# A decoder's cross-attention rearranged: relative context from memory, scores in eight array blocks, probabilities normalised on GpSimd, one ring of four banks

## The chip, the cores and the metric

One core of one Trainium2 chip runs the whole program. It has TensorE (PE, with its weight loads as PEld), VectorE (DVE), ScalarE (ACT), GpSimd (POOL) and SyncE (SP), whose queue issues the DMAs. The metric is the device time of the program in microseconds (us). Each engine takes its instructions in their written order and waits on semaphores; the engines run beside each other.

## The reference

The reference is a chain of twelve blocks on a state x of 32 sequences with 32 queries and 256 features, and a context of 32 sequences with 257 keys. The change lies in block four, a decoder of six layers, and in a preparation that it puts into block one. Each decoder layer is self-attention over 32 queries, cross-attention over the 257 keys and an MLP, each with a residual and a layer norm:

```
def proj(x, w, b):
    y = x @ w + b
    ...
q = proj(xq, W[0], B[0])
k = proj(xkv, W[1], B[1])
v = proj(xkv, W[2], B[2])
score = jnp.einsum('bhqd,bhkd->bhqk', q, k) / math.sqrt(DH)
attn = jax.nn.softmax(score, axis=-1)
out = jnp.einsum('bhqk,bhkd->bhqd', attn, v)
```

There are 16 heads of 16 features. All is float32.

## The kernel before

**The decoder's pipeline.** The 32 sequences lie in NG = 8 tiles of GB = 4 sequences (128 rows of queries). Six layers by eight tiles make 48 positions. The outer loop (decoder_layers, L2092) takes 51 steps; in step s the self-attention of position s, the projections ("prep": queries q, keys K, values V) of position s-1, the cross-attention of position s-2 and the output projection, norm and MLP of position s-3 are worked on together. A step has U = 8 units, u0 to u7, and the table UNIT_JOBS says which jobs PE does in which unit: S0, S1q, S1k, S2, S3, S6, S7 are self-attention, Y is the cross-attention's output projection, D0 to D3 are the MLP, n is a transpose. X and XK are done once a layer for the last key. Each job writes one bank of a ring of four PSUM banks (RING, RB = 4), ACT or DVE empties it, and job n waits until job n-4 has been emptied.

**Cross-attention.** A unit is one sequence and half of the heads. In each even unit `scores` makes the scores of two units (a pair) in banks 0 and 1; DVE takes their maxima (`maxima`), ACT takes four exponentials with their sums (`exponentials`). Two units later PE transposes the probabilities into a bank of its own (TURN), ACT copies that bank to pT (`copy_transposed`), and in odd units `values` multiplies with V into bank PV. The 257th key is kept out of the 256-key tiles: its part is handled by subtracting its key from the others (a bias less_last on K) and by its own share. After every fourth unit DVE computes the reciprocals of the sums and spreads them over a 512-wide tile (`reciprocals`), PE turns that into per-query factors with eight records of matmul (the L2363 matmuls), and DVE applies them to the heads (`own_heads`, five instructions).

**Order.** The DVE's order inside a unit is written out in its loop: jobs put off from the unit before (S3, D3), maxima, self_shares in u4, the unit's jobs, reciprocals, own_heads, own_queries in u2, self_shift in u3, then the second half of a layer norm (norm_apply), which waits for POOL's power of -1/2. A layer norm's first half (norm_statistics) empties the bank with its first instruction. POOL does nothing in the decoder but two tiny instructions a norm. ACT takes the first job of an even unit ahead of the exponentials.

**Names.** mm is a matmul, tr a transpose through PE. A float32 matmul shows as two PE records. ps is PSUM in eight banks; E.ctx holds two tiles of context, E.h the state.

```
[("D2", 1, "act"), ("X", None, "act")],
[("S7", None, "dve"), ("D3", None, "dve")],
```

These are u6 and u7 of the table.

## Time and profile before

| what | us |
|---|---|
| median of 3 runs | 4367.97 (4359.14 to 4368.52) |
| the profiled execution, first to last instruction | 4363.9 |
| PE busy in it | 3907.7 (90%) |
| DVE busy | 2607.3 (60%) |
| ACT busy | 1849.2 (42%) |
| POOL busy | 308.2 (7%) |

The profiled span lies 4.1 us under the median. The first self-attention transpose of the decoder starts at 718.11 us and its last MLP matmuls at 2716.80 us, so the decoder is the longest block, nearly half of the time. Busy time of PE overlaps between neighbours, because matmuls are pipelined; the distance between two starts tells what a job costs there.

### The profile page before, as it was taken

What the parts mean: (1) busy time and instruction counts of PE and PEld (TensorE: products, weight loads), DVE (VectorE), ACT (ScalarE), POOL (GpSimd) and SP (SyncE); (2) the same over time, 40 slices, a digit from 0 to 9 for tenths busy, and PEclk for the clock granted to TensorE, in tenths of its full rate; (3) what the DMA queues carried; (4) which work ended last, traced back from release to release, by engine and by line L of the source; (5) the groups of instructions that cost most, each with busy time, mean ns of one, the idle gap of its engine ahead of it and who ended that gap; (6) DMA issues with size and microseconds to landing.
All of it is one profiled execution on the core that took longest, in us unless ns stands there. A gap on an engine that the chain in (4) does not pass through costs nothing. (4 is left out here: it accounts for less than half of the span.)

```text
span 4363.9 us, 103007 instructions
## 1 busy us (share of the span) xinstructions
PE 3907.7 (90%) x43004; PEld 2910.7 (67%) x43004; DVE 2607.3 (60%) x5439; ACT 1849.2 (42%) x5103; POOL 308.2 (7%) x560
## 2 busy tenths in 40 slices
PE   7988995999999999999999997859678879889867
PEld 6765984677777777777777776548545569555535
DVE  3436113777777777777877775641156757346535
ACT  1221321455444544545445444312166736246523
POOL 0000101000000000000000000020111100000000
PEclk9999997999999999999999999969899979899978
DMA  4110484001111111111101100028654410000000
GB/s 155 60 63 3 152 301 158 30 31 52 50 35 48 50 36 47 51 34 48 59 26 47 60 21 11 11 82 288 213 165 146 156 44 1 26 30 30 11 1 12
DMA packets 116924, 310.60 MB, mean 71 GB/s; under 512 B 29352, under 2 KB 75624, under 8 KB 92016
## 3 DMA queue, kind: packets, MB, share of 16 engines
q1 hardware_dynamic: 113392, 295.61, 19.9%
q0 software_dynamic: 3072, 8.39, 0.5%
q8 instruction: 345, 5.65, 0.5%
q14 instruction: 115, 0.94, 0.1%
HBM read 289.01 MB, written 14.94 MB: 70 GB/s over the span
## 5 line engine op out<-in xcount | busy, mean ns | idle before, releaser
L2578 ACT COPY layers_pT<-banks 128x512 f32<-128x512 f32 x384 | 227.3, 592 | 554.5 <-PE banks L2346 553.8
L2277 PE MATMUL banks<-weights_a,ctx_tiles 128*128 128x256 f32 x1536 | 363.8, 380 | 0.0
L2270 PE MATMUL banks<-ctx_tiles,weights_a 128*128 128x512 f32 x768 | 363.4, 596 | 0.0
L2571 ACT ACTIVATE layers_probs<-banks,layers_negmax 128x256 f32<-128x256 f32 x768 | 354.2, 480 | 13.9 <-DVE layers_negmax L2436 6.8
L2277 PEld LDWEIGHTS banks<-weights_a,ctx_tiles 128*128 128x128 f32 x1536 | 285.9, 191 | 75.8 <-issue 46.4
L2414 DVE TENSOR_TENSOR layers_V<-banks,rows_a 128x512 f32<-128x512 f32 x192 | 132.7, 691 | 221.2 <-PE banks L2277 217.2
L2346 PE MATMUL banks<-const,layers_probs 128*128 128x128 f32 x1536 | 244.6, 282 | 2.8 <-ACT layers_pT L2578 2.8
L2346 PEld LDWEIGHTS banks<-const,layers_probs 128*128 128x128 f32 x1536 | 171.6, 141 | 106.4 <-issue 96.5
L2435 DVE TENSOR_REDUCE layers_negmax<-banks 128x4 f32<-128x1024 f32 x192 | 233.8, 1218 | 4.0 <-PE banks L2338 3.9
L2538 ACT ACTIVATE layers_KT<-banks,layers_less_last 128x256 f32<-128x256 f32 x384 | 162.1, 480 | 157.1 <-PE banks L2270 157.1
L2338 PE MATMUL banks<-layers_KT,layers_qblk 32*64 32x256 f32 x3072 | 211.3, 389 | 0.0
L2270 PEld LDWEIGHTS banks<-ctx_tiles,weights_a 128*128 128x128 f32 x768 | 132.1, 192 | 92.7 <-issue 92.6
L2321 PE MATMUL banks<-layers_dm_nT,weights_b 128*128 128x128 f32 x1536 | 190.0, 278 | 0.6 <-ACT layers_dm_nT L2533 0.6
L2321 PEld LDWEIGHTS banks<-layers_dm_nT,weights_b 128*128 128x128 f32 x1536 | 181.9, 195 | 0.9 <-ACT layers_dm_nT L2533 0.9
L2326 PE MATMUL banks<-weights_b,layers_hid 128*128 128x256 f32 x768 | 176.9, 384 | 3.8 <-ACT layers_hid L2561 3.1
L2326 PEld LDWEIGHTS banks<-weights_b,layers_hid 128*128 128x128 f32 x768 | 142.7, 190 | 36.6 <-issue 18.2
L2571 ACT ACTIVATION_READ_ACCUMULATOR layers_probs<-banks,layers_negmax 128x1 f32 x768 | 162.6, 212 | 0.0
L2338 PEld LDWEIGHTS banks<-layers_KT,layers_qblk 32*64 32x64 f32 x3072 | 98.6, 132 | 73.5 <-issue 40.6
L2561 ACT ACTIVATE layers_hid<-banks,layers_dm_cols 128x128 f32<-128x128 f32 x384 | 110.5, 379 | 62.3 <-PE banks L2321 62.2
L2358 PE MATMUL banks<-layers_pT,layers_V 128*32 128x64 f32 x6144 | 125.5, 222 | 6.1 <-ACT layers_pT L2578 6.1
L2859 PE MATMUL banks<-weights_a,ctx_tiles 128*128 128x512 f32 x256 | 127.2, 625 | 2.5 <-ACT l2x_nT L3083 1.5
L2358 PEld LDWEIGHTS banks<-layers_pT,layers_V 128*32 128x32 f32 x6144 | 96.2, 110 | 46.8 <-issue 40.0
(715 smaller groups left out, 8268.5 us busy)
## 6 DMA issues: line engine op xcount, KB each, us to landing
ctx_tiles<-in_ctx SPq DMA_DIRECT2D x65, 1028.0 KB, 5.3
weights_a<-in_L_w SPq DMA_DIRECT2D x44, 1024.0 KB, 5.5
l2x_B<-positions SPq DMA_DIRECT2D x32, 1280.0 KB, 5.9
weights_b<-in_L_w SPq DMA_DIRECT2D x32, 1024.0 KB, 6.2
weights_c<-in_L_w SPq DMA_DIRECT2D x16, 1024.0 KB, 7.1
weights_b<-in_L_xattn_w SPq DMA_DIRECT2D x12, 1024.0 KB, 7.4
l0x_key_rows<-in_ctx_rows SPq DMA_DIRECT2D x32, 256.0 KB, 2.6
ctx_tiles<-in_ctx_keys SPq DMA_DIRECT2D x32, 256.0 KB, 2.7
```

The source lines that it names most:

```text
L2270: last = mm(o.rearrange("p (j k) -> p j k", j=2), ca_wk[:, c, m * P:(m + 1) * P], keys, start=c == 0, stop=c == DC - 1)
L2277: last = mm(o[:, b * D:(b + 1) * D], E.ctx[:, tile % 2, c, first:first + P], ca_wv[:, c], start=c == 0, stop=c == DC - 1)
L2321: last = mm(o[:, i * P:(i + 1) * P], dm_w1[:, c, m * P:(m + 1) * P], dm_nT[:, c], start=c == 0, stop=c == DC - 1)
L2326: last = mm(o[:, 0:D], hid[:, m], dm_w2[:, m], start=m == 0, stop=m == FC - 1)
L2338: last = mm(ps[half, r // 2, a * KW:(a + 1) * KW], qblk[rows, tile % 2, cc, j + a], KT[rows, tile % 2, cc, (j + a) * KW:(j + a + 1) * KW], ...
L2346: last = tr(ps[:, TURN, (KC * t + c) * P:(KC * t + c + 1) * P], probs[:, cc, j, t, c * P:(c + 1) * P], E.c("ident"))
L2358: last = mm(ps[32 * i:32 * (i + 1), PV, j * 64:(j + 1) * 64], V[:, pos % 2, KC * j + c, cc * P + 32 * i:cc * P + 32 * (i + 1)], pT[:, k % ...
L2414: last = v.tensor_tensor(V[:, tile % 2, KC * arg:KC * (arg + 1)], o.rearrange("p (b d) -> p b d", b=KC), E.rA[:, 0].unsqueeze(1).to_broadc ...
L2435: link(v.tensor_reduce(peak, ps[:, 0:2].rearrange("p t (a x) -> p t a x", a=2), AX.X, ALU.max, negate=True))
L2538: last = a(KT[:, pos % 2, m, j * KW:(j + 1) * KW], o[:, j % 2 * KW:(j % 2 + 1) * KW], ACT.Identity, bias=less_last[:, pos // NG % 2, m, se ...
L2571: a(probs[:, cc, i, t], ps[:, t, i % 2 * KW:(i % 2 + 1) * KW], ACT.Exp, bias=negmax[:, cc, t, i:i + 1], accum_out=totals[:, cc, t, i:i + 1 ...
L2578: nc.scalar.copy(pT[:, k % 4].rearrange("p t c x -> p (t c x)"), ps[:, TURN]).then_inc(s["copied"], 1)
```

## The change

Five things are done together.

- The relative context. In block one (joint_attention) POOL subtracts the last key from the 256 others, tile by tile (less_last), and SP writes the result to a scratch tensor in memory (ctx_rel). The decoder loads its tiles from there, from step 0 on. The bias less_last of K and its job XK go, K is emptied by one instruction of 512 columns instead of two of 256, and V is copied without a bias row, since the values are relative too.
- The scores. The four strips of 32 rows write four banks, and the two sequences of a pair write the two halves of the rows, so that the eight matmuls of a pair have eight blocks of the array (4 strips by 2 halves), where before they had four, used twice.
- The normalising. For every pair DVE adds and inverts the sums (pair_rates) and POOL multiplies the probabilities with them before they are transposed (scale, twice a pair). The spread tile, its matmuls and the two multiplications of the heads go; own_heads is two instructions of half the width, once a pair.
- The ring. The scores have banks 0 to 3; transposes (T) and values (PV) become jobs of the ring of four banks 4 to 7 with all other jobs. A PV is emptied by DVE in the next unit, behind the maxima.
- POOL's order is written out anew: the roots of the norms stand between the scales.

```diff
-                    if K >= GB and K % GB == 1:
+                    if K % GB == 3:
+                        g = K // GB
+                        sp.wait_ge(s["rel_ready"], g + 1)
+                        sp.dma_start(E.ctx_rel[g], rel[:].rearrange("p c j k -> p c (j k)")).then_inc(s["rel_stored"], 16)
+                    if K >= GB and K % GB == 1 and (K + 3) // GB < NG:
...
+                    tile = E.ctx[:, g % 2].rearrange("p c (j k) -> p c j k", j=GB)
+                    for c in range(DC):
+                        last = nc.gpsimd.tensor_tensor(rel[:, c], tile[:, c, :, 1:LK], tile[:, c, :, 0:1].to_broadcast([P, GB, KW]), ALU.subtract)
+                    last.then_inc(s["rel_ready"], 1)
...
-    TURN, PV, RING, RB = 2, 3, 4, 4
+    RING, RB = 4, 4
...
         for step, parts in enumerate(steps):
             for u in range(U):
+                it = step * U + u
+                if ca_unit(it - 2):
+                    at[it - 2 - 2 * U, "T", None] = len(jobs)
+                    jobs.append((step, u, "T", it - 2, "act"))
                 for kind, arg, engine in UNIT_JOBS[u]:
...
+                if u % 2 and ca_unit(it - 3):
+                    at[(it - 3) // 2 - U, "PV", None] = len(jobs)
+                    jobs.append((step, u, "PV", it - 3, "dve"))
...
-                        sp.dma_start(E.ctx[:, step % 2], A["ctx"][step % NG]).then_inc(s[f"ctx{step % 2}"], 16)
+                        sp.dma_start(E.ctx[:, step % 2, :, 0:GB * KW], E.ctx_rel[step % NG]).then_inc(s[f"ctx{step % 2}"], 16)
...
                     need(pe, "exp_done", 2 * k)
+                    for r in range(4):
+                        rows = slice(32 * r, 32 * (r + 1))
+                        for a in range(2):
+                            last = mm(ps[64 * a:64 * (a + 1), r, 0:KW], qblk[rows, tile % 2, cc, j + a], KT[rows, tile % 2, cc, (j + a) * KW:(j + a + 1) * KW], start=True, stop=True)
+                    last.then_inc(s["scores_done"], 1)
+
+                def transposes(o, k, pos, cc, j):
+                    pe.wait_ge(s["scaled"], k + 1)
...
-                        for r in (0, 2, 1, 3):
-                            rows, half = slice(32 * r, 32 * (r + 1)), slice(64 * (r % 2), 64 * (r % 2 + 1))
-                            last = mm(ps[half, r // 2, a * KW:(a + 1) * KW], qblk[rows, tile % 2, cc, j + a], KT[rows, tile % 2, cc, (j + a) * KW:(j + a + 1) * KW], start=True, stop=True)
...
+                    link(v.scalar_tensor_tensor(blend[:], both[:, :, 0], E.c("pairmask")[:, 0:1], last_share, ALU.mult, ALU.add))
+                    v.scalar_tensor_tensor(attnT[:, cc, j * LQ:(j + 2) * LQ].rearrange("p (j q) -> p j q", j=2), both[:, :, 1], E.c("pairmask")[:, 1:2], blend[:], ALU.mult, ALU.add).then_inc(s["evac_dve"], 1)
...
                     for a in put_off:
-                        take(*a)
-                    put_off.clear()
+                        if a[3] != "PV":
+                            take(*a)
                     if it % 2 == 0 and ca_unit(it):
                         maxima(*ca_unit(it))
+                    for a in put_off:
+                        if a[3] == "PV":
+                            take(*a)
+                    put_off.clear()
                     if u == 4 and steps[step]["sa"] is not None:
                         self_shares(steps[step]["sa"])
+                    if it % 2 and ca_unit(it - 1):
+                        pair_rates(*ca_unit(it - 1))
...
+                def scale(k, pos, cc, j):
+
+                    pool.wait_ge(s["rates_ready"], k // 2 + 1)
+                    at = slice(2 * (j % 2), 2 * (j % 2) + 2)
+                    nc.gpsimd.tensor_tensor(probs[:, cc, j // 2, at], probs[:, cc, j // 2, at], rates[:, cc, j // 2, at].unsqueeze(2).to_broadcast([P, 2, KW]), ALU.mult).then_inc(s["scaled"], 1)
+
+                for it in range(N * U + 1):
+                    step, u = it // U, it % U
+                    if u == 0 and step and steps[step - 1]["dm"] is not None:
+                        root("dm")
+                    if u == 2 and step < N and steps[step]["out"] is not None:
+                        root("ca")
+                    if u == 7 and steps[step]["sa"] is not None:
+                        root("sa")
+                    if it % 2 and ca_unit(it - 1):
+                        scale(*ca_unit(it - 1))
+                        scale(*ca_unit(it))
```

**DVE from u7 into u1, before.** y_sa is the norm behind S7, y_dm the norm behind D3, negmax the maxima, V the emptying of job V.

```order
L2385 TENSOR_TENSOR layers_y_sa<-banks,rows_c 128x256 [waits layers_job_done]
...
L2396 TENSOR_SCALAR layers_y_sa<-layers_y_sa,layers_stats_sa 128x256 [waits layers_power_ready]
...
L2385 TENSOR_TENSOR layers_y_dm<-banks,rows_b 128x256 [waits layers_job_done]
...
L2435 TENSOR_REDUCE layers_negmax<-banks 128x2x2 [waits layers_scores_done]
...
L2414 TENSOR_TENSOR layers_V<-banks,rows_a 128x512 [waits layers_job_done]
L2441 TENSOR_TENSOR layers_rates<-layers_totals,layers_last_e 128x2x4 [waits layers_last_exp,layers_exp_done]
```

The same place now; blend and attnT are own_heads, rates is pair_rates.

```order
L2462 TENSOR_TENSOR layers_rates<-layers_totals,layers_last_e 128x4 [waits layers_last_exp,layers_exp_done]
...
L2401 TENSOR_TENSOR layers_y_sa<-banks,rows_c 128x256 [waits layers_job_done]
...
L2401 TENSOR_TENSOR layers_y_dm<-banks,rows_b 128x256 [waits layers_job_done]
...
L2454 TENSOR_REDUCE layers_negmax<-banks 128x4 [waits layers_scores_done]
...
L2472 SCALAR_TENSOR_TENSOR layers_blend<-banks,const,layers_last_v 128x64 [waits layers_job_done]
...
L2433 COPY layers_V<-banks 128x512 [waits layers_job_done]
```

A wait for the exponentials of the same unit pair now stands ahead of the norm of S7, and the emptying of PV stands between the maxima and V.

**PE from u7 into u0, now.** Line 2372 is the transposes T, 2353 is D3, 2383 is PV, 2365 the scores, 2302 is K, 2309 is V.

```order
L2353 MATMUL banks<-weights_b,layers_hid 128x256 [waits layers_evac_act]
...
L2383 MATMUL banks<-layers_pT,layers_V 32x64 [waits layers_evac_act]
...
L2365 MATMUL banks<-layers_KT,layers_qblk 64x256 [waits layers_exp_done,layers_evac_act,layers_qblk_ready]
...
L2372 MATMUL banks<-const,layers_probs 128x128 [waits layers_scaled,layers_evac_act]
...
L2302 MATMUL banks<-ctx_tiles,weights_a 128x512 [waits layers_ctx0,layers_evac_dve]
...
L2309 MATMUL banks<-weights_a,ctx_tiles 128x256 [waits layers_evac_dve]
```

T now waits for POOL (layers_scaled), K for the emptying of D3 and V for that of PV, both by DVE; before, T waited for the exponentials and for its own bank.

**POOL, one step, now.**

```order
L188 TENSOR_SCALAR layers_stats_sa<-layers_stats_sa 128x1 [waits layers_var_ready]
L193 TENSOR_TENSOR layers_stats_sa<-layers_stats_sa,const 128x1 [waits layers_added_eps]
L2539 TENSOR_TENSOR layers_probs<-layers_probs,layers_rates 128x512 [waits layers_rates_ready] x2
L188 TENSOR_SCALAR layers_stats_dm<-layers_stats_dm 128x1 [waits layers_var_ready]
L193 TENSOR_TENSOR layers_stats_dm<-layers_stats_dm,const 128x1 [waits layers_added_eps]
```

The two scales of the last pair of a step stand behind the root of S7's norm.

## Rows read from the trace of the kernel before

**Rows 1.** Busy time by engine (PE, PEld, DVE, ACT, POOL), clock, DMA, one decoder step.
```profile
1499.60:1540.02 40.42, 40.40 (x459) 29.72 (x459) 31.51 (x70) 20.12 (x66) 2.48 (x6) 1.00 0.09 28
```

**Rows 2.** Timeline of PE: start, us, line, operation, records; the same step.
```profile
1504.05 1.06 PE L2262 MATMUL banks<-layers_sa_nT,weights_c 128*128 128x128 f32 x8
...
1507.87 0.66 PE L2358 MATMUL banks<-layers_pT,layers_V 128*32 128x64 f32 x32
1508.34 0.61 PE L2363 MATMUL banks<-layers_spread,const 128*32 128x256 f32 x8
1508.88 1.09 PE L2338 MATMUL banks<-layers_KT,layers_qblk 32*64 32x256 f32 x16
1509.91 0.66 PE L2346 MATMUL banks<-const,layers_probs 128*128 128x128 f32 x4
...
1513.98 1.07 PE L2301 MATMUL banks<-weights_a,layers_sa_k 128*32 128x256 f32 x16
...
1523.05 1.03 PE L2295 MATMUL banks<-weights_c,layers_sa_nT 128*128 128x256 f32 x4
...
1533.17 0.60 PE L2346 MATMUL banks<-const,layers_probs 128*128 128x128 f32 x4
...
1534.65 3.69 PE L2326 MATMUL banks<-weights_b,layers_hid 128*128 128x256 f32 x16
1538.28 0.66 PE L2358 MATMUL banks<-layers_pT,layers_V 128*32 128x64 f32 x32
1538.86 1.09 PE L2338 MATMUL banks<-layers_KT,layers_qblk 32*64 32x256 f32 x16
1539.88 0.66 PE L2346 MATMUL banks<-const,layers_probs 128*128 128x128 f32 x4
...
1542.31 1.89 PE L2277 MATMUL banks<-weights_a,ctx_tiles 128*128 128x256 f32 x8
```

**Rows 3.** Timeline of DVE in the same step.
```profile
1504.42 0.16 DVE L2441 TENSOR_TENSOR layers_rates<-layers_totals,layers_last_e 128x8 f32<-128x8 f32 x1
...
1504.85 0.17 DVE L2443 TENSOR_TENSOR layers_rates<-layers_rates,layers_last_e 128x8 f32<-128x8 f32 x1
...
1505.66 0.41 DVE L2396 TENSOR_SCALAR layers_y_dm<-layers_y_dm,layers_stats_dm 128x256 f32<-128x256 f32 x1
...
1506.91 2.47 DVE L2410 SCALAR_TENSOR_TENSOR weights_a<-banks,layers_sa_cols,const 128x1024 f32<-128x1024 f32 x2
...
1519.12 0.69 DVE L2414 TENSOR_TENSOR layers_V<-banks,rows_a 128x512 f32<-128x512 f32 x1 [0.41 <-PE banks L2277]
...
1521.87 1.22 DVE L2435 TENSOR_REDUCE layers_negmax<-banks 128x4 f32<-128x1024 f32 x1
...
1534.67 0.42 DVE L2385 TENSOR_TENSOR layers_y_sa<-banks,rows_c 128x256 f32<-128x256 f32 x1 [1.34 <-PE banks L2314]
...
1537.23 0.41 DVE L2396 TENSOR_SCALAR layers_y_sa<-layers_y_sa,layers_stats_sa 128x256 f32<-128x256 f32 x1 [0.99 <-POOL layers_stats_sa L193]
...
1538.48 0.41 DVE L2385 TENSOR_TENSOR layers_y_dm<-banks,rows_b 128x256 f32<-128x256 f32 x1
...
1540.02 1.22 DVE L2435 TENSOR_REDUCE layers_negmax<-banks 128x4 f32<-128x1024 f32 x1
```

**Rows 4.** Timeline of ACT: the end of the exponentials of the last pair.
```profile
1536.18 0.25 ACT L2573 ACTIVATE layers_last_e<-layers_negmax 128x8 f32<-128x8 f32 x1
```

**Rows 5.** POOL by line and form: count, busy us, mean ns, idle before.
```profile
L3033 POOL TENSOR_TENSOR ctx_tiles<-ctx_tiles 128x512 f32<-128x512 f32 x32 | 37.2, 1183 | 40.8 <-DMA ctx_tiles<-in_ctx_keys 40.7 <-DMA ctx_tiles<-in_ctx_last 0.2
```

**Rows 6.** Timeline of POOL and DVE in block seven, side by side.
```profile
3228.20 4.34 POOL L3033 TENSOR_TENSOR ctx_tiles<-ctx_tiles 128x512 f32<-128x512 f32 x3
3228.27 1.12 DVE L182 TENSOR_SCALAR l2x_n<-x_state,l2x_stats 128x256 f32<-128x256 f32 x1 [1.00 <-POOL l2x_stats L193]
...
3275.77 3.04 POOL L3033 TENSOR_TENSOR ctx_tiles<-ctx_tiles 128x512 f32<-128x512 f32 x3
```

**Rows 7.** Timeline of PE early in the decoder.
```profile
806.37 0.43 PE L2358 MATMUL banks<-layers_pT,layers_V 128*32 128x64 f32 x16 [2.22 <-ACT layers_pT L2578]
806.73 1.98 PE L2338 MATMUL banks<-layers_KT,layers_qblk 32*64 32x256 f32 x16
```

More of the change, by code:

```diff
@@ L2447, in own_heads, with pair_rates @@
-                def own_heads(k, pos, cc, j):
+                def pair_rates(k, pos, cc, j):
+                    dve.wait_ge(s["exp_done"], 2 * k + 4)
+                    dve.wait_ge(s["last_exp"], k // 2 + 1)
+                    rate = rates[:, cc, j // 2]
+                    link(v.tensor_tensor(rate, totals[:, cc, j // 2], last_e[:, cc, j // 2], ALU.add))
+                    v.reciprocal(rate, rate).then_inc(s["rates_ready"], 1)
+                def own_heads(o, n, k, pos, cc, j):
                     tile = pos % NG
-                    dve.wait_ge(s["pv_done"], k + 1)
-                    dve.wait_ge(s["shares_done"], k // GB + 1)
-                    if k % (NG * U) == GB - 1:
+                    if k % (NG * U) == 0:
@@ L2513, in _, with root @@
             def _(pool):
-                n = 0
-                for parts in steps:
-                    for part, kind in (("out", "ca"), ("sa", "sa"), ("dm", "dm")):
-                        if parts[part] is not None:
-                            power(E, pool, s, n, stats[kind][:, 8:9], stats[kind][:, 7:8], 1e-12)
-                            n += 1
+                made = [0]
+                def root(kind):
+                    power(E, pool, s, made[0], stats[kind][:, 8:9], stats[kind][:, 7:8], 1e-12)
+                    made[0] += 1
+                def scale(k, pos, cc, j):
[13 more added lines that the diff above has]
+                        scale(*ca_unit(it))
             @blk.scalar
@@ L2582, in _ @@
                     early = 0
-                    if ca_unit(it - 2):
-                        copy_transposed(*ca_unit(it - 2))
                     if it % 2 == 0 and ca_unit(it):
-                        while jobs_in(it)[early:early + 1] and early < 1 + (jobs_in(it)[0][3] == "XK"):
-                            take(*jobs_in(it)[early])
-                            early += 1
+                        early = 1 + (jobs_in(it)[0][3] == "T")
+                        for b in jobs_in(it)[0:early]:
+                            take(*b)
                         exponentials(*ca_unit(it))
```

196 lines of the change are left out of this document (85 added, 111 removed).

## The prediction

> **What bounds the kernel now.** I read the busy time by stretch first. In a decoder step of 40.42 us PE is busy 40.40, DVE 31.51, ACT 20.12 and POOL 2.48, with the full clock [rows 1]. So PE alone sets the step; what matters is the distance between two PE starts. The decoder has 45 steps in which all four parts are at work (steps 3 to 47), each of this length. Then I read PE, DVE and ACT of that step by time, because the order on DVE and the four banks decide whether PE can keep its pace. The reader is to see in [rows 2, 3] that PE has no gap, and that DVE is ahead of PE in u7 (it waits 1.34 us for S7) but behind it elsewhere: it starts the maxima of u4 at 1521.87, and PE has been at the next work for a while.
>
> **PE work that goes.** The spread matmuls cost 1508.88 - 1508.34 = 0.54 us, twice a step: 1.08 [rows 2]. The scores cost 1509.91 - 1508.88 = 1.03 us, four times a step [rows 2]. They are 16 records of 256 columns in four blocks. D3's 16 records of the same length in the whole array take 1538.28 - 1534.65 = 3.63, or 0.227 each [rows 2]; a quarter of that is 0.91, so 0.12 of the 1.03 is change-over. Eight blocks need 0.45 + 0.12, about 0.6. The bounds are 0.6 and 1.03 (no gain); I take 0.6, since four blocks already come to a quarter, here and in S3. That saves 4 x 0.43 = 1.72. All of this is on the path. With no new wait the step is 40.4 - 2.8 = 37.6 us. T and PV have as many records as before. XK is six small jobs and counts as nothing.
>
> **DVE, ACT, POOL.** DVE loses two reciprocals with spread a step, 1505.66 - 1504.42 = 1.24 each [rows 3], and two own_heads of five instructions of 128x128, each 0.3 by the same bounds as below: about 5.5. It gains four pair_rates of 0.43 (1504.42 to 1504.85 is an add and a reciprocal [rows 3]) and four own_heads of about 0.6 (two instructions of 128x64, each between the 0.16 of 8 elements and the 0.41 of 256; I take 0.3). That is 1.4 less. But it has to be there at certain times. POOL gets eight scales a step. The nearest rows are 32 subtractions of the same form, mean 1.18 us, and three in a row take 3.04, so 1.04 each when alone [rows 5, 6]. ACT has fewer instructions for K and two more last_e; it has 20 us to spare.
>
> **A walk through the step.** I set t = 0 at the start of the scores in u0 and carry every wait on. Hand-overs to PE count 0.15.
>
> *The last pair.* D2 ends 1538.86 - 1533.17 = 5.69 before the scores. The last exponential of u6 ends at 1536.43 [rows 4], 3.26 behind D2: t = -2.4. pair_rates waits for this, ahead of S7 in DVE's order, and ends at -2.0; before, DVE was at S7 already. From the start of S7's statistics to the second half of the norm is 1537.23 - 1534.67 = 2.56 [rows 3]: root done at 0.5. POOL's scale of unit 6 stands behind that root and runs 0.5 to 1.55. PE is at T at 0.6 and waits until 1.65: **1.1 us**.
>
> *The shared access.* The three instructions of the norm start at the same moment as the scales. [Rows 6] show what then happens: a tensor_scalar of 128x256 takes 1.12 us instead of the 0.41 of [rows 3], as it ends just behind the POOL instruction, and three POOL instructions take 4.34 instead of 3.04. So they take turns: scale 6, tensor_scalar to 1.65, scale 7 to 2.65, the other two to 3.45. The norm alone would take 1538.48 - 1537.23 = 1.25 and end at 1.8.
>
> The Trainium skill (SBUF — State Buffer, Who interferes with whom) says that a DVE instruction with two SBUF inputs, or in a two-port mode, and a GpSimd instruction that reads SBUF exclude each other for the whole instruction. By that rule the trace agrees; without it, with each at its own length, the step would be 42.7 instead of 44.6 (worked out below).
>
> *K and V of u0.* K0 needs D3's bank, four jobs back, emptied by the first instruction of its statistics at 3.45 + 0.42. PE would be there at 1.65 + 0.7 = 2.4 and starts at 4.0: **1.6 us**. The statistics end at 5.0 (1540.02 - 1538.48 = 1.54), the maxima with their clamp at 6.4, own_heads at 7.0. V0 needs the bank of PV. PE would be there at 4.0 + 1.7 = 5.7 and starts at 7.15: **1.4 us**.
>
> *u1.* V0 ends at 8.9. DVE copies it (0.85 with hand-over), does the MLP's norm (1.25), pair_rates (0.43) and S1q's emptying (2.47): 13.9. PV in u1 is four jobs behind S1q. PE would be there 0.44 for T and 1507.87 - 1504.05 = 3.82 behind V0, at 13.15: **0.9 us**.
>
> *u4.* S2 is four jobs behind the PV of u3. From the end of Y to S2 PE needs 1523.05 - 1513.98 less the 0.43 of the scores: 8.6. DVE needs 0.1 + 2.56 + 1.25 for Y's norm, 0.8 for S3, 0.43 for the rates, 0.65 for V2, 2.2 for the shift (V2 to maxima is 1521.87 - 1519.12 = 2.75 in all [rows 3]), 1.4 for the maxima and 0.6 for own_heads: 10.0, and 0.15. That is 1.5 us of wait; two of the shift's instructions meet the scales, which adds about 0.3, and T of u4 waits 0.25 for its scale: **2.0 us**.
>
> Waits: 1.1 + 1.6 + 1.4 + 0.9 + 2.0 = 7.0 us against 2.8 saved. The step is 40.4 + 4.2 = **44.6 us**. Over 45 steps this is 45 x 4.2 = 189 us. The steps at the ends lack either self-attention or keys and have slack of their own; I count them as nothing, within 10 us.
>
> Without the taking of turns the waits are 1.1 + 0 + 1.5 + 0.9 + 1.6 = 5.1, the step 42.7, and the sum 45 x 2.3 = 104 us.
>
> **What costs nothing.** In block one 16 POOL subtractions of 128x1024, some 2 us each by twice the form of [rows 5], lie beside PE, which sets that block's pace; POOL has only a root for each tile there, and the next root stands ahead of each subtraction. SP's new wait for rel_ready stands ahead of the loads of key rows, which are three deep, and eight stores of 1 MB go out in some 260 us. Without that cover it would be 8 x 4 us. The decoder's first context load is now issued with step 0 and used some 20 us later. At step ends the same SP queue as before loads weights; its share is 0.09 [rows 1]. I take 0, and up to 15 us for the upper end.
>
> **Rivals.**
> 1. *The waits without taking turns.* For: POOL's two short instructions beside DVE in a decoder step cost almost nothing now. Against: [rows 6]. 4368 + 104 = 4472.
> 2. *The scores stay at 1.03.* For: no row has 32*64 tiles of 256 columns in eight blocks. Against: the quarter above. Half of the lost 1.72 hides behind DVE (in u0 and u4, where PE waits anyway), so 45 x 0.86 = 39 more: 4596.
> 3. *The clock falls.* After a gap of 2.22 us the scores took 1.98 instead of 1.09, at 1.2 instead of 2.4 GHz [rows 7]. If the gaps of u0, 4 us in 7, do this once a step, some 2 us are added: 45 x 2 = 90 more, 4647. Against: my single gaps are all under 2.
> 4. *Faster.* DVE, with 1.4 us less work, is early enough at one place, the run from S7 in u7 to S1q in u1. If the norm of S7, the maxima and PV come early there, the banks are free when PE arrives. It decides at a shortening of that run by about 5 us, the sum of its four waits. Then PE keeps nearly all of the 2.8: 4368 - 126 = 4242. For: DVE would be busy 30 of 37.6 us only. Against: the run is a chain, with the exponentials and a root of 1.0 us in it, that no spare time elsewhere shortens.
> 5. *A draw.* The waits come to 2.8 by being half as long as I say: 4368.
>
> **How the numbers follow.** The profiled span is 4363.9, 4.1 under the median; I add the change to the median: 4368 + 189 = 4557. Chances: forecast 0.40, rival 1 0.24, rival 2 0.07, rival 3 0.07, rival 4 0.15, rival 5 0.07. The range from 4400 to 4640 holds the forecast and rivals 1 and 2 with their ends, and leaves out rivals 4 and 5 and most of 3. About 0.2% (9 us) is what a measurement of this kernel can tell. Faster 0.15, same 0.06, slower 0.79.
>
> **What would show it.** Right: a decoder step of 44 to 45 us with PE busy some 38; PE idle before T in u0 by POOL, and before K0, V0, PV of u1 and S2 by DVE; scores 0.6 us apart from T; the norm of S7 stretched from 1.25 to nearly 3 us beside two scales. The walk is wrong if PE's gaps sum to under 3 us a step, if the rates of the last pair are done before S7 ends, or if a scale takes other than 1.0 to 1.2 us where DVE is quiet. If the stretch is missing, rival 1 holds.

## The result and the profile after

The changed kernel takes 4499.31 us, the median of 4 runs (4494.44 to 4504.27), against 4368.25 (4359.14 to 4370.86) for the kernel before on the same chip: a ratio of 1.0307, 95% interval [1.0296, 1.0319]. The change makes the kernel 131 us slower. The profiled execution has a span of 4492.7 us, 128.8 more than before. The forecast was 4557, the range 4400 to 4640.

The first two lines of the profile's page after, and then two full decoder steps by stretch (length; busy PE, PEld, DVE, ACT, POOL; granted clock; DMA share), which answer to [rows 1]:

```profile
span 4492.7 us, 101679 instructions
...
PE 3846.5 (86%) x42188; PEld 2843.7 (63%) x42188; DVE 2577.7 (57%) x5343; ACT 1824.7 (41%) x4995; POOL 729.7 (16%) x960
```
```profile
1506.43:1550.48 44.05, 40.37 (x449) 28.80 (x442) 30.68 (x66) 19.69 (x64) 10.64 (x15) 0.96 0.32 106
1550.48:1593.98 43.50, 38.84 (x450) 28.23 (x443) 30.67 (x66) 19.69 (x64) 10.65 (x15) 1.00 0.08 25
```

PE was busy for the whole step before. Now it is idle for 4.7 us of 43.5 in the second step, which has the full clock. The first lost clock (0.96) and is 0.55 us longer. From the scores of u0 in step 3 to those in step 48 a step is 43.67 us on average, where it was 40.62: 3.05 x 45 = 137 us. The rest of the difference lies elsewhere: the decoder's first PE instruction comes 7.2 us later than before, the steps at the decoder's ends give 5 back, and what follows its last MLP matmuls is 10 us shorter (1637 instead of 1647). The change touches nothing there, and in the traces of all the kernels below this part takes between 1637 and 1651 us, so these 10 us are no effect that is shown.

The second step on PE (start, duration, in brackets the idle time and its releaser), which answers to [rows 2]:

```profile
1550.48 0.69 PE L2365 MATMUL banks<-layers_KT,layers_qblk 32*64 32x256 f32 x16
1552.09 0.63 PE L2372 MATMUL banks<-const,layers_probs 128*128 128x128 f32 x4 [0.92 <-POOL layers_probs L2539]
1552.56 0.38 PE L2288 MATMUL banks<-const,h_state 128*128 128x128 f32 x2
1554.12 1.98 PE L2302 MATMUL banks<-ctx_tiles,weights_a 128*128 128x512 f32 x4 [1.18 <-DVE layers_y_dm L2401]
1557.08 1.99 PE L2309 MATMUL banks<-weights_a,ctx_tiles 128*128 128x256 f32 x8 [0.97 <-DVE layers_attnT L2473]
...
1563.74 0.65 PE L2383 MATMUL banks<-layers_pT,layers_V 128*32 128x64 f32 x32 [0.51 <-DVE weights_a L2429]
1564.33 0.69 PE L2365 MATMUL banks<-layers_KT,layers_qblk 32*64 32x256 f32 x16
1564.94 0.66 PE L2372 MATMUL banks<-const,layers_probs 128*128 128x128 f32 x4
...
1575.96 1.88 PE L2302 MATMUL banks<-ctx_tiles,weights_a 128*128 128x512 f32 x4
1578.90 1.13 PE L2322 MATMUL banks<-weights_c,layers_sa_nT 128*128 128x256 f32 x4 [1.05 <-DVE layers_attnT L2473]
```

These are the only waits of the step: T, K0 and V0 of u0, PV of u1, S2 of u4. The brackets sum to 4.6 us. The distances between starts say more. From each I take the distance of the same two jobs in a kernel without these waits (below, "and ScalarE's order"). S0 to K0, for one, is 1.56 here and 0.22 there. By this T waits 1.00 us, K0 1.35, V0 1.24, PV 0.58 and S2 1.22, in all 5.4. The scores stand 1564.94 - 1564.33 = 0.61 us ahead of T, where it was 1.03.

DVE in the same step, which answers to [rows 3], with POOL's two scales:

```profile
1548.16 0.16 DVE L2462 TENSOR_TENSOR layers_rates<-layers_totals,layers_last_e 128x4 f32<-128x4 f32 x1 [3.35 <-ACT layers_last_e L2603]
...
1548.45 0.40 DVE L2401 TENSOR_TENSOR layers_y_sa<-banks,rows_c 128x256 f32<-128x256 f32 x1
...
1550.97 1.12 DVE L2412 TENSOR_SCALAR layers_y_sa<-layers_y_sa,layers_stats_sa 128x256 f32<-128x256 f32 x1 [1.00 <-POOL layers_stats_sa L193]
1552.13 1.14 DVE L2413 TENSOR_TENSOR layers_y_sa<-layers_y_sa,rows_c 128x256 f32<-128x256 f32 x1
1553.31 0.42 DVE L2414 TENSOR_TENSOR h_state<-layers_y_sa,rows_c 128x256 f32<-128x256 f32 x1
1553.65 0.42 DVE L2401 TENSOR_TENSOR layers_y_dm<-banks,rows_b 128x256 f32<-128x256 f32 x1
...
1555.12 1.19 DVE L2454 TENSOR_REDUCE layers_negmax<-banks 128x4 f32<-128x1024 f32 x1
```
```profile
1550.91 2.08 POOL L2539 TENSOR_TENSOR layers_probs<-layers_probs,layers_rates 128x512 f32<-128x512 f32 x2
```

DVE waits 3.35 us for the last exponential, although the bank of S7, its next piece of work, has been full since 1546.3, when PE ended this:

```profile
1545.23 1.03 PE L2341 MATMUL banks<-weights_c,layers_sa_attnT 128*128 128x256 f32 x4
```

So some 1.9 of the 3.35 us delay S7. Then the norm of S7 meets the scales. Its first two instructions take 1.12 and 1.14 us. Over the whole program those lines have a mean of 1090 and 1113 ns for this norm and of 413 and 425 for the norm behind Y, which meets no scale.

### The profile page after: what moved, and what is told of

The parts are those of the page before. It is cut to its first block and busy times, and to the rows that moved or that the text cites. A ratio compares the mean times of both kernels' runs of the same rounds, so it can differ in the third digit from the quotient of the medians.

```text
span 4492.7 us, 101679 instructions
## 1 busy us (share of the span) xinstructions
PE 3846.5 (86%) x42188; PEld 2843.7 (63%) x42188; DVE 2577.7 (57%) x5343; ACT 1824.7 (41%) x4995; POOL 729.7 (16%) x960
## 5 line engine op out<-in xcount | busy, mean ns | idle before, releaser
L2539 POOL TENSOR_TENSOR layers_probs<-layers_probs,layers_rates 128x512 f32<-128x512 f32 x384 | 393.3, 1045 | 694.3 <-DVE layers_rates L2463 694.3
L2302 PE MATMUL banks<-ctx_tiles,weights_a 128*128 128x512 f32 x768 | 390.9, 634 | 52.0 <-DVE layers_y_dm L2401 52.0
L2372 PE MATMUL banks<-const,layers_probs 128*128 128x128 f32 x1536 | 243.5, 282 | 43.7 <-POOL layers_probs L2539 42.4
L2433 DVE COPY layers_V<-banks 128x512 f32<-128x512 f32 x192 | 132.7, 691 | 244.7 <-PE banks L2309 241.4
L2579 ACT ACTIVATE layers_KT<-banks,layers_key_bias 128x512 f32<-128x512 f32 x192 | 132.7, 691 | 154.4 <-PE banks L2302 154.2
L2365 PE MATMUL banks<-layers_KT,layers_qblk 32*64 32x256 f32 x3072 | 133.4, 403 | 0.0
```

The costliest lines, as they stand in the source:

```text
L2302: last = mm(o, ca_wk[:, c, m * P:(m + 1) * P], E.ctx[:, tile % 2, c, 2 * i * KW:2 * (i + 1) * KW], start=c == 0, stop=c == DC - 1)
L2365: last = mm(ps[64 * a:64 * (a + 1), r, 0:KW], qblk[rows, tile % 2, cc, j + a], KT[rows, tile % 2, cc, (j + a) * KW:(j + a + 1) * KW], star ...
L2372: last = tr(o[:, (KC * i + c) * P:(KC * i + c + 1) * P], probs[:, cc, j // 2, 2 * (j % 2) + i, c * P:(c + 1) * P], E.c("ident"))
L2433: last = v.tensor_copy(V[:, tile % 2, KC * arg:KC * (arg + 1)], o.rearrange("p (b d) -> p b d", b=KC))
L2539: nc.gpsimd.tensor_tensor(probs[:, cc, j // 2, at], probs[:, cc, j // 2, at], rates[:, cc, j // 2, at].unsqueeze(2).to_broadcast([P, 2, KW ...
```

## The experiments

The times are medians of 4 runs (the last row 12); the ratio is to runs of the kernel before on the same chip, with its 95% interval. The kernel before took 4368 us on the chips of most rows and 4361.7 on that of "and ScalarE's order", "the same, four blocks" and the last row. The last column is the time in the trace from the first to the last MLP matmul of the decoder (D3), which is 47 steps.

| kernel | us | ratio to before | D3 to D3, us |
|---|---|---|---|
| before | 4368 | 1 | 1875.5 |
| the change | 4499.3 | 1.0307 [1.0296, 1.0319] | 2012.1 |
| GpSimd scales first | 4457.9 | 1.0213 [1.0196, 1.0231] | 1972.9 |
| S7 first | 4401.3 | 1.0080 [1.0064, 1.0097] | 1914.3 |
| no scaling | 4424.4 | 1.0132 [1.0114, 1.0150] | 1940.6 |
| fill instead of scaling | 4458.9 | 1.0209 [1.0191, 1.0226] | 1968.7 |
| scaling on ScalarE | 4435.6 | 1.0148 [1.0127, 1.0170] | 1943.2 |
| scores in four blocks | 4537.2 | 1.0395 [1.0375, 1.0416] | 2047.3 |
| new order on DVE | 4340.6 | 0.9942 [0.9924, 0.9960] | 1853.0 |
| and scaling on ScalarE | 4315.6 | 0.9886 [0.9868, 0.9905] | 1826.3 |
| and ScalarE's order | 4250.8 | 0.9735 [0.9714, 0.9756] | 1765.7 |
| the same, four blocks | 4328.9 | 0.9917 [0.9894, 0.9940] | 1836.2 |
| the same, scaling on GpSimd | 4302.0 | 0.9853 [0.9831, 0.9875] | 1814.6 |
| before, with block one's part | 4367.6 | 1.0007 [0.9996, 1.0018] | 1875.6 |

The theory from the prediction: the step is set by a run over DVE and POOL from S7 in u7 to the emptying of S1q in u1; it starts late, behind the rates, and is stretched by taking turns with the scales. The rivals: the change costs by work wherever it is done; the stretch has another cause; the clock does it.

### GpSimd scales first

```
                     if it % 2 and ca_unit(it - 1):
                         scale(*ca_unit(it - 1))
                         scale(*ca_unit(it))
+                    if u == 7 and steps[step]["sa"] is not None:
+                        root("sa")
```
(and `root("sa")` no longer ahead of the scales)

> The changed kernel with one order turned round: in unit 7 GpSimd scales the probabilities of units 6 and 7 first and takes the power for the self-attention's norm after them. Times are on the clock of one step of the changed kernel's trace (scores of unit 0 at 1550.48). The wait of the transposes for GpSimd (0.92 us a step) must go in every theory. Theory (GpSimd's scaling and VectorE's instructions with two operands in memory take turns): scaling now lies at 1548.5 to 1550.6, beside the statistics of S7 instead of the norm; those are stretched, the power is at 1551.5 to 1552.3, the norm ends at about 1553.7 as now, and the ring bank of D3, for which K waits, comes free no earlier: 0 to 15 us faster. Rival (no taking turns; the norm was long for another reason): statistics end at 1550.0, power at 1551.4, norm ends at 1552.8, V starts 0.8 us earlier, 45 x 0.8 = 36 us faster or more.

Measured: 41 us faster than the change. My number was wrong, and the rival's was right for a wrong reason. In the trace (start, duration) the scales now lie beside the statistics of S7:

```profile
1488.42 2.22 POOL L2539 TENSOR_TENSOR layers_probs<-layers_probs,layers_rates 128x512 f32<-128x512 f32 x2 [7.41 <-DVE layers_rates L2463]
1488.69 1.06 DVE L2403 TENSOR_TENSOR layers_y_sa<-layers_y_sa,h_state 128x256 f32<-128x256 f32 x1
1489.78 0.43 DVE L2404 BATCH_NORM_STATS2 layers_stats_sa<-layers_y_sa 128x6 f32<-128x256 f32 x1
```

They do get in each other's way: L2403, which adds two tiles in memory, takes 1.06 us instead of the 0.42 it has elsewhere, and the two scales 2.22 instead of 2.04. But that is the only one of the four statistics with both operands in memory. I had counted all four instructions of the statistics as stretched. V0 starts 5.89 us behind the scores instead of 6.60; 0.71 x 45 = 32 us, and 8 more come from the clock (below).

### S7 first

```
-                    if it % 2 and ca_unit(it - 1):
+                    if it % 2 and u != 7 and ca_unit(it - 1):
                         pair_rates(*ca_unit(it - 1))
                     for a in jobs_in(it):
...
+                    if u == 7 and ca_unit(it - 1):
+                        pair_rates(*ca_unit(it - 1))
```

> The changed kernel with one order turned round on VectorE: in unit 7 it takes the statistics of S7 (ready at 1546.3) before the rates of units 6 and 7, which wait for ScalarE's last exponential until 1548.16. Theory (the run from S7's statistics over the power, the norm, D3, the maxima to the values' bank sets V's start in unit 0, and everything in it is late because the statistics wait behind the rates): statistics 1546.5 to 1548.1, power done 1548.7, norm beside the scaling until 1551.6, D3's bank free at 1552.1, values' bank at 1555.1, V at 1555.3 instead of 1557.08: 1.8 us a step, 45 x 1.8 = 80 us faster, about 4420 us. Rival (ScalarE's or GpSimd's part, not the order on VectorE, sets the unit): V's start moves by under 0.4 us, under 18 us faster.

Measured: 98 us faster. This is the largest effect of one edit. The statistics start when PE has S7 ready, and the rates hardly wait:

```profile
1507.40 0.42 DVE L2401 TENSOR_TENSOR layers_y_sa<-banks,rows_c 128x256 f32<-128x256 f32 x1 [1.50 <-PE banks L2341]
...
1509.27 0.16 DVE L2462 TENSOR_TENSOR layers_rates<-layers_totals,layers_last_e 128x4 f32<-128x4 f32 x1 [0.30 <-ACT layers_last_e L2605]
...
1511.59 0.69 PE L2365 MATMUL banks<-layers_KT,layers_qblk 32*64 32x256 f32 x16
...
1516.07 1.99 PE L2309 MATMUL banks<-weights_a,ctx_tiles 128*128 128x256 f32 x8 [0.97 <-DVE layers_attnT L2473]
```

V0 starts 4.48 us behind the scores of u0 instead of 6.60, which is 95 us over 45 steps. The norm is as stretched as before (1.12 and 1.14 us); it only starts earlier. So the late start is worth more than the stretch: leaving the scales out, which takes away the stretch and T's wait, gives 75 us (next experiment). The waits of V0, PV and S2 remain.

### No scaling, and a fill in its place

The first leaves the scaling out. The second puts a fill of equal length in its place; in both the probabilities stay unnormalised.

```
-                    pe.wait_ge(s["scaled"], k + 1)
+                    pe.wait_ge(s["rates_ready"], k // 2 + 1)
```
```
-                    nc.gpsimd.tensor_tensor(probs[:, cc, j // 2, at], probs[:, cc, j // 2, at], rates[:, cc, j // 2, at].unsqueeze(2).to_broadcast([P, 2, KW]), ALU.mult).then_inc(s["scaled"], 1)
+                    if k:
+                        pool.wait_ge(s["scaled"], k)
+                    nc.gpsimd.memset(idle[:], 0.0).then_inc(s["scaled"], 1)
```

> The changed kernel without GpSimd's scaling of the probabilities: the 384 multiplications are left out and the transposes wait for the rates instead, so the probabilities stay unnormalised. Theory (taking turns stretches the norm from 1.25 to 2.7 us, and the norm stands ahead of D3's statistics and all that follows): no wait of the transposes in unit 0, norm 1.3 us, K at 1552.8, V at 1555.65 instead of 1557.08: 1.4 us a step, about 64 us faster. Rival (norm would be as long without the scaling): V's start stays, and only the wait in front of the transposes is handed to K: 0 to 10 us faster.

> The changed kernel with each of GpSimd's 384 scalings replaced by a fill of 1070 elements a partition on a tile of its own: about as long (the fill of 706 elements of block one took 0.686 us), with the same waits, but it reads nothing in memory; the probabilities stay unnormalised. It parts the duration of GpSimd's step from its reading. Theory (it is the reading and VectorE's two operands that exclude each other): the transposes still wait about 1 us in unit 0, but the norm is 1.3 us, and V starts at 1555.65: some 60 us faster, as without the scaling. Rival (any work of GpSimd on memory stretches the norm, or its length alone counts): norm 2.7 us as before, 0 to 10 us faster.

Measured: 75 us faster without scaling, 40 with the fill. The norm of S7 without scaling, then with the fill, where POOL's line stands first:

```profile
1523.52 0.41 DVE L2412 TENSOR_SCALAR layers_y_sa<-layers_y_sa,layers_stats_sa 128x256 f32<-128x256 f32 x1 [1.00 <-POOL layers_stats_sa L193]
1523.97 0.43 DVE L2413 TENSOR_TENSOR layers_y_sa<-layers_y_sa,rows_c 128x256 f32<-128x256 f32 x1
```
```profile
1494.87 2.10 POOL L2542 MEMSET layers_idle<- 128x1070 f32 x2
1494.96 1.05 DVE L2413 TENSOR_SCALAR layers_y_sa<-layers_y_sa,layers_stats_sa 128x256 f32<-128x256 f32 x1 [1.00 <-POOL layers_stats_sa L193]
...
1496.04 0.43 DVE L2414 TENSOR_TENSOR layers_y_sa<-layers_y_sa,rows_c 128x256 f32<-128x256 f32 x1
```

Nothing on POOL, no stretch: the cause is the scale. The fill, which reads nothing, still delays the tensor_scalar (1.05 us) but not the tensor_tensor with two operands in memory (0.43, while the second fill runs). So my expectation was half right: there are two ways of being in each other's way, and the fill leaves one of them. V0 starts 5.16 us behind the scores without scaling and 5.81 with the fill, against 6.60: 65 and 36 us, and in both some 8 more for the clock (below), so 73 and 44 of the 75 and 40 measured.

The Trainium skill (SBUF — State Buffer, Who interferes with whom) says that a DVE instruction with two SBUF inputs contends with a GpSimd instruction that reads SBUF and not with one that only writes. The tensor_tensor agrees: 1.14 us beside the scale, 0.43 beside the fill. Of a two-port mode, which it says a tensor_scalar can enter, it says that it contends with GpSimd, without that exception. The tensor_scalar's 1.12 and 1.05 us fit this; that it runs in such a mode no row here shows.

### The same work on ScalarE

```
+                def scale(k, pos, cc, j):
+                    act.wait_ge(s["rates_ready"], k // 2 + 1)
+                    for r in range(2 * (j % 2), 2 * (j % 2) + 2):
+                        last = a(probs[:, cc, j // 2, r], probs[:, cc, j // 2, r], ACT.Copy, scale=rates[:, cc, j // 2, r:r + 1])
+                    last.then_inc(s["scaled"], 1)
```
(called for both units of a pair at the end of an odd unit; POOL's is gone)

> The changed kernel in its own order, with the normalising alone moved from GpSimd to ScalarE (four copies with a scale per pair of units at the end of the odd units). All the work of the change is there, but GpSimd does none of it. Theory (the scaling costs by GpSimd's access to memory and by its place on the path, not by the work): as without any scaling, about 4424 us, 75 us faster than the change. Rival (the scaling costs wherever it is done): 4480 us or more.

Measured: 64 us faster than the change, most of the 75 us that leaving the scaling out gave. Four copies take 1.71 us together. The rival that the work costs wherever it is done falls: a full decoder step is 42.06 us long with the scaling on ScalarE and 42.06 without any, and the stretch from D3 to D3 differs by 2.6 us. Of the 11 us between the two times 9 lie behind the decoder in the two traces (1651 and 1642 us), where the kernels are the same.

### Scores in four blocks

```
+                            part = slice(32 * (2 * (r // 2) + a), 32 * (2 * (r // 2) + a + 1))
-                            last = mm(ps[64 * a:64 * (a + 1), r, 0:KW], qblk[rows, tile % 2, cc, j + a], KT[rows, tile % 2, cc, (j + a) * KW:(j + a + 1) * KW], start=True, stop=True)
+                            last = mm(ps[64 * a:64 * (a + 1), r, 0:KW], qblk[part, tile % 2, cc, j + a], KT[part, tile % 2, cc, (j + a) * KW:(j + a + 1) * KW], start=True, stop=True)
```
(which strip of rows a matmul takes now follows from the half that it writes, so the scores come out of the wrong rows)

> The changed kernel with the scores' matmuls spread over four blocks of the array instead of eight: the rows that a matmul takes are chosen by which half of the bank it writes, so two follow each other on every block; the scores are wrong by that, their number and size are not. It prices the eight blocks. The scores should take 1.03 us instead of 0.62. Theory (that time lies on the path in units 2 and 6 alone; in unit 0 it is hidden by the transposes' wait and in unit 4 by S2's): 2 x 0.41 x 45 = 37 us slower, about 4536 us. Rival (TensorE's time counts in full in each unit): 4 x 0.41 x 45 = 74 us slower, 4573 us. Rival (eight blocks are no faster than four): no difference.

Measured: 38 us slower. The scores are 1.03 us ahead of T again:

```profile
1531.07 1.11 PE L2366 MATMUL banks<-layers_KT,layers_qblk 32*64 32x256 f32 x16
1532.10 0.66 PE L2373 MATMUL banks<-const,layers_probs 128*128 128x128 f32 x4
```

Eight blocks do save 0.41 us, but only half of that shortens the step: in u0 and u4 PE would wait anyway. A step at the full clock is 44.33 us long instead of 43.49, which is two times 0.42. T's wait for POOL shrank from 42.4 to 23.6 us over the program, or 0.4 a step, which is what the scores grew by. That the total meets the 37 us expected so closely is partly luck: with T's wait shorter the clock fell in 4 steps instead of 17 (see rival 3 below), so the 45 full steps grew by 30 us only, and the rest lies outside them.

### A new order on DVE

```
                     for a in put_off:
-                        if a[3] != "PV":
-                            take(*a)
+                        take(*a)
+                    put_off.clear()
                     if it % 2 == 0 and ca_unit(it):
                         maxima(*ca_unit(it))
-                    for a in put_off:
-                        if a[3] == "PV":
-                            take(*a)
-                    put_off.clear()
+                    for a in unfinished:
+                        norm_apply(*a)
+                    unfinished.clear()
```
(and S7 ahead of the rates, as above)

> The changed kernel with VectorE's order written anew, nothing else: the statistics of S7 ahead of the rates in unit 7 (as in the run before), the values of every second unit taken out of their bank ahead of the maxima instead of behind them, and the norm behind D3 applied ahead of V's copy in unit 0, where VectorE waits for V anyway, instead of behind it. Theory (TensorE waits only because the ring banks are emptied late by VectorE): on top of the 98 us of the order in unit 7, the waits left in that trace go, V in unit 0 (1.2 us), PV in unit 1 (0.6) and S2 (1.1): 2.9 us x 45 = 130 us more, about 4270 us, faster than the kernel before by some 2%. Rival (each wait taken away uncovers another, such as the exponentials, which now start 0.6 us later, or the scores' banks): half of it at most, 4330 us or more.

Measured: 61 us faster than with S7 first alone, 27 faster than the kernel before (ratio 0.9942). All waits for DVE went, but the rival holds in part: the maxima of u0 end 4.4 us behind the scores instead of 3.9, so 0.5 us later, ScalarE's exponentials with them, and K's banks are emptied behind those. This edit moves two things beside S7 and takes three waits away (V0, PV, S2); which of the two took which is argued and not shown. Of PE in this kernel, K in u1 and V in u5:

```profile
1496.47 1.98 PE L2302 MATMUL banks<-ctx_tiles,weights_a 128*128 128x512 f32 x4 [0.55 <-ACT layers_KT L2580]
...
1517.30 1.99 PE L2309 MATMUL banks<-weights_a,ctx_tiles 128*128 128x256 f32 x8 [0.61 <-ACT layers_KT L2580]
```

### Scaling on ScalarE in the new order, and ScalarE's order

> The kernel of the run before with the normalising moved from GpSimd to ScalarE: four copies with a scale per pair of units, at the end of the odd units of ScalarE's order. Theory (GpSimd's scaling costs by stretching the norm beside it, and after the reordering only K's wait of 0.3 us in unit 0 is left of that): 5 to 15 us faster than with GpSimd, about 4255 us, if ScalarE's copies take 0.35 us each. Rival (ScalarE's queue becomes the late one: 4 x 0.35 us more in each odd unit, ahead of the next unit's evacuations): 10 to 50 us slower than with GpSimd.

Measured: 25 us faster than with the new order alone, more than expected. In unit 1 K's wait went, and T of u2 waits for its scaling instead; V in u5 waits as before:

```profile
1510.69 1.99 PE L2309 MATMUL banks<-weights_a,ctx_tiles 128*128 128x256 f32 x8 [0.61 <-ACT layers_KT L2571]
...
1533.44 0.63 PE L2372 MATMUL banks<-const,layers_probs 128*128 128x128 f32 x4 [0.45 <-ACT layers_probs L2600]
```

The next kernel moves two things on ScalarE:

```
-                        early = 1 + (jobs_in(it)[0][3] == "T")
+                        early = (2 if u == 4 else 1) + (jobs_in(it)[0][3] == "T")
```
(K's evacuation ahead of the exponentials in u4; and in u1 both `scale` calls directly behind the copy of T)

> The kernel with the new order on VectorE and the normalising on ScalarE, with two places of ScalarE's order changed: in unit 1 the scaling stands ahead of K's evacuation, in unit 4 K's evacuation stands ahead of the exponentials. In the trace of the run before, TensorE still waited for ScalarE in two places a step: 0.5 us ahead of the transposes of unit 2 (their scaling stood behind the evacuations of unit 1) and 0.8 us ahead of V in unit 5 (K's bank was emptied behind the exponentials). Theory: both go and nothing comes up, since ScalarE waits idle where the moved instructions now stand: 1.3 x 45 = 58 us faster, about 4257 us; TensorE busy for 37.6 us of a step of about 37.8. Rival (the exponentials or the maxima come up next): under 30 us faster.

Measured: 4250.8 us, 65 faster than the one before it, 2.65% faster than the kernel before and 5.5% than the change. Its step:

```profile
1495.92:1533.87 37.95, 37.93 (x450) 28.30 (x443) 29.61 (x67) 26.14 (x80) 2.48 (x6) 1.00 0.09 30
```

PE is busy for 37.93 of 37.95 us. All the arithmetic of the change is in this kernel; what differs from the change is the order on two engines and that ScalarE does the scaling.

### The same kernel with four blocks, and with GpSimd's scaling

> The kernel of the run before with the scores in four blocks of the array instead of eight, chosen by the half of the bank (the scores are wrong by that, number and size are not). In the changed kernel this cost 38 us, because half of the units hid it behind waits. Theory (without waits TensorE's time counts in full): 4 x 0.41 x 45 = 74 us slower than the kernel with eight blocks. Rival (the waits were not what hid it): 38 us again.

Measured: 78 us slower than with eight blocks, of 74 expected. Where PE waits for nothing its time counts in full, twice as much as in the change.

> The fastest kernel so far (VectorE's new order, K's evacuation of unit 4 ahead of the exponentials) with the normalising given back to GpSimd. It prices GpSimd's place beside VectorE where TensorE waits for nothing else. Theory (the scaling stretches the norm of S7 by 1.45 us, so the maxima of unit 0, the exponentials and K's evacuation behind them come later, and K of unit 1 waits 0.55 us for its bank, as in the trace of the new order with GpSimd; K of unit 0 waits 0.2): 0.75 x 45 = 34 us slower than with ScalarE, about 4285 us. Rival (with this order nothing is left of it): within 10 us of the kernel with ScalarE, 4251 us.

Measured: 51 us slower than with ScalarE. T's, V's and S2's waits stay away, and K of u1 waits:

```profile
1521.43 1.98 PE L2302 MATMUL banks<-ctx_tiles,weights_a 128*128 128x512 f32 x4 [0.56 <-ACT layers_KT L2580]
```

I had used the bracket as the price. By the distances between starts, against the kernel with ScalarE, K of u1 waits 0.73 us and K0 0.19. Each of these two K also takes 0.10 us longer to the next start (1.82 instead of 1.72). Together this is 1.1 us a step (39.06 instead of 37.95), or 50 of the 51 us.

### Block one's part alone

```
+                def less_last(g):
...
+                        last = nc.gpsimd.tensor_tensor(rel[:, c], tile[:, c, :, 1:LK], tile[:, c, :, 0:1].to_broadcast([P, GB, KW]), ALU.subtract)
```
(with the stores of `rel` and their waits, added to the kernel before)

> The kernel before, with the part of the change that lies in block one alone: GpSimd subtracts the last key (16 instructions) and SyncE stores the eight tiles, which nothing reads. The decoder is as before. Theory (block one's end came 6.9 us later in the changed kernel's trace, because GpSimd's power for the next norm stands behind less access to memory beside its subtractions, and TensorE lost the clock there): 7 us slower, 4375 us. Rival (what was later in block one is chance of the clock at its start): 0 to 2 us slower.

Measured: a ratio of 1.0007 [0.9996, 1.0018] over 12 runs, so between 2 us faster and 8 slower. It doesn't tell 7 us from none. In its one trace the decoder's first PE instruction is at 725.83 us, as in the changed kernel (725.3) and not as before (718.1). In the traces of all thirteen kernels with this part it lies between 723.5 and 731.7 us. That speaks for a delay of 5 us or more, but there is one trace only of the kernel before, and the times do not prove it.

## Why the prediction came out as it did

**Sign and mechanism were right.** The order of waits, their releasers and their places came out as listed. T's wait and most of K0's went with one exchange on DVE ("S7 first"), and those of V0, PV and S2 with two more, done together.

**PE work.** The scores came to 0.61 us instead of the 0.6 taken. The step without waits is 37.95, not 37.6. Most of the error is in the spread matmuls, priced at their own distance of 0.54 us [rows 2]; the scores' 4 x 0.41 instead of 4 x 0.43 is 0.08 of it. PV is followed by the spread after 1508.34 - 1507.87 = 0.47 us and by scores after 1538.86 - 1538.28 = 0.58 [rows 2], so leaving the spread out moves the scores by only 0.54 + 0.47 - 0.58 = 0.43, and 0.86 a step goes, not 1.08. With 4 x 0.41 this is 2.5.

**The last pair and the shared access.** From the scores at t = 0 the last exponential ended at -2.43 (-2.4 said), the rates at -1.95 (-2.0), the root at 0.46 (0.5), T started at 1.61 (1.65), the stretched norm ended at 3.25 (3.45).

**K0, V0, PV.** Starts at 3.64, 6.60 and 13.26, where I had 4.0, 7.15 and 14.05. The waits are 1.35, 1.24 and 0.58 instead of 1.6, 1.4 and 0.9. Each term was a little long: hand-overs on DVE overlap (D3's statistics start 0.08 us ahead of the norm's recorded end), and durations were added up with none of that.

**u4: the term that was mis-sized most.** 1.2 instead of 2.0. T did not wait, and the shift was not stretched, since what meets the scale in u3 is the copy under a mask and a reduction:

```profile
1574.77 0.79 DVE L2486 COPY_PREDICATED_SCALAR layers_sa_sc<-mask_zero,layers_floor 128x512 f32 x1
1575.59 0.69 DVE L2487 TENSOR_REDUCE layers_sa_max<-layers_sa_sc 128x16 f32<-128x512 f32 x1
1576.31 0.69 DVE L2488 TENSOR_TENSOR layers_sa_sc<-layers_sa_sc,layers_sa_max 128x512 f32<-128x512 f32 x1
```
```profile
1574.08 2.04 POOL L2539 TENSOR_TENSOR layers_probs<-layers_probs,layers_rates 128x512 f32<-128x512 f32 x2 [2.33 <-DVE layers_rates L2463]
```

The first takes 0.79 us here and a mean of 0.78 without any scaling, and the subtraction starts as the scales have ended. "Two of the shift's instructions meet the scales" was right, that it adds 0.3 was not. With T's 0.25 this is 0.55 of the 0.8; the rest I have not taken apart.

**The sum.** The waits are 5.4 instead of 7.0 and the savings 2.5 instead of 2.8. V0 and S2, which start behind a wait, also take 0.1 us longer each to the next start, which no term had. So a step at the full clock grew from 40.42 to 43.49, by 3.07. Two more terms were missing. The lost clock adds 0.18 to the average step. And the prediction's "each of this length" is wrong for 6 of the 45 steps of the kernel before. Step 3, with its lost clock, took 42.04 us, and in five steps X and XK come on top, eight records each. Here are step 8 and, with them, step 9:

```profile
1010.46:1050.89 40.43, 40.41 (x466) 29.73 (x459) 31.50 (x69) 20.13 (x66) 2.47 (x6) 1.00 0.33 93
1050.89:1092.75 41.86, 41.86 (x481) 31.51 (x474) 31.25 (x69) 21.48 (x72) 2.48 (x6) 1.00 0.08 27
```

These six add 0.20 us to the average step before. In the change step 3 is no longer than the others (43.47), XK is gone, and a step with X is 0.6 us longer and the next one 0.6 shorter (44.07 and 42.90 at the full clock), so nothing of the 0.20 is left. XK with X, counted as nothing, was worth 5 x 1.44 = 7 us. In all 3.07 + 0.18 - 0.20 = 3.05 us a step instead of 4.2, so 137 instead of 189 us.

**Rival 1** is refuted by the norm's rows, with the scales and without them. Its time (4472) was nearer to the 4499 measured than mine (4557), so the total does not speak for the taking of turns; it had the waits too small and missed the clock, where mine had them too large. **Rival 2** is refuted by the 0.61. **Rival 3** happened, but small. I argued that my single gaps are all under 2 us; the clock fell behind gaps of 0.92 and 1.18 us. In the step at 1506.43 the granted clock was 0.60 from 1510 to 1514 and K took 3.10 us instead of 1.98, that is, part of it ran at 1.2 instead of 2.4 GHz:

```profile
1508.04 0.63 PE L2372 MATMUL banks<-const,layers_probs 128*128 128x128 f32 x4 [0.92 <-POOL layers_probs L2539]
...
1510.07 3.10 PE L2302 MATMUL banks<-ctx_tiles,weights_a 128*128 128x512 f32 x4 [1.18 <-DVE layers_y_dm L2401]
1513.02 2.56 PE L2309 MATMUL banks<-weights_a,ctx_tiles 128*128 128x256 f32 x8
```
```profile
1510.00:1514.00 4.00, 3.93 (x6) 1.66 (x7) 2.79 (x8) 1.50 (x7) 0.79 (x2) 0.60 0.00 0
```

V0 would have started at 1513.03 anyway, so K's 1.12 us were hidden and the step grew by only 0.55. The clock fell in 17 of the 45 full steps, and the average step is 0.18 above the full-clock one: 8 us in all, where the rival had 90. With GpSimd scaling first, with S7 first, without scaling and with the fill the clock is at 1.00 from step 4 to step 47, so each of these got some 8 us on top. **Rival 4** did not happen, but its counter-argument was wrong. I wrote that the run from S7 is a chain that no spare time elsewhere shortens. Exchanging two steps on DVE shortened it by 2.1 us a step. Of the 248 us between the change and the kernel of 4251 us, 197 came from the order on DVE and ScalarE and 51 from the place of the scaling.

**What costs nothing.** SP's waits and the context loads show no wait of PE. Block one's part was taken as 0. It is 7 us in two traces against one, and not certain in the times.

## What to carry over

Work taken off the bound engine pays only where no other engine's order decides, so walk the others' order against the new pace and look for an instruction that waits at the head of its queue while the next one's data are ready. Taking S7 ahead of such a wait (3.35 us for the last exponential) gave 98 us; leaving the added work out gave 75. Put GpSimd's work beside VectorE instructions that it doesn't stretch, or give it to ScalarE where that has time. Read the trace again after each edit: the new order on DVE brought up a wait for K's bank, and the scaling on ScalarE behind it one of T.

## What the hardware showed unexpectedly

- A fill on GpSimd, which reads nothing, stretches a 128x256 tensor_scalar on VectorE from 0.41 to 1.05 us, and leaves a tensor_tensor with two operands in memory at 0.43. A scale, which reads too, stretches both (1.12 and 1.14 us).
- A copy under a mask of 128x512 (0.79 us) and V's copy out of its bank (0.69) are not stretched by a scale beside them.
- Sixteen records of 32x64 and 256 columns take 0.61 us in eight blocks and 1.03 in four.
- The four matmuls of K take 1.98 us behind a wait and 1.88 without one. The bracket of a wait is less than its price by the distance between starts, here by 0.1 to 0.3 us each.
- The granted clock was 0.60 from 1510 to 1514 us behind two idle stretches of PE of 0.92 and 1.18 us. It stayed at 1.00 in the step at 1550.48 with two just as long, and in 28 of the 45 full steps in all.
